# Two layers of attention and mixture of experts on one Trainium2 core: the second attention's output projected inside its own loop

## What is computed

```python
h = _layernorm(x) * (1 + ca) + sa
x = x + ga * _L1_attn_ref(h, w_qkvw, w_out)     # second layer's attention
h = _layernorm(x) * (1 + cb) + sb
x = x + gb * _L1_ffn_ref(h, Wr, br, W1, W2)     # one of 8 experts for each row

def _L1_attn_ref(x, w_qkvw, w_out):
    qkvw = x @ w_qkvw
    ...
    attn = jax.nn.softmax(q @ k.swapaxes(-2, -1) * scale, axis=-1)
    o = (attn @ v).swapaxes(1, 2).reshape(B, S, dim)
    return o * w.reshape(B, S, dim) @ w_out
```

## Time and profile before

| | |
|---|---|
| median of 3 executions | 2002.04 us (2001.77 to 2004.55) |
| the profiled execution | 2007.54 us, of which the span from first to last instruction is 2005.8 us |
| first attention and set-up | to 431 us |
| rows of the first layer, routing | 431 to 509 us |
| experts of the first layer | 509 to 1112 us |
| merge | to 1205 us |
| loop of the second attention | 1205 to 1588 us |
| tail and rows of the second layer | 1588 to 1691 us |
| routing, experts, end | 1691 to 2006 us |

### The profile page before, as it was taken

How to read it: one execution, slowest core, us unless ns; L and a number is a source line. 1 busy time by engine, 2 the same in 40 slices (tenths; PEclk the granted TensorE clock), 3 DMA queues, 4 the chain that set the end, 5 groups by cost and what they waited for, 6 DMA issues and landing times.

```text
span 2005.8 us, 32138 instructions
## 1 busy us (share of the span) xinstructions
PE 1682.2 (84%) x11048; PEld 1009.5 (50%) x11048; DVE 1160.1 (58%) x1885; ACT 861.2 (43%) x1909; POOL 1073.5 (54%) x901
## 2 busy tenths in 40 slices
PE   5699999976899999999999368777776476899992
PEld 3355555544466666666666233232231154677771
DVE  6798898876223223233233687999999687222214
ACT  3444444334344444444444374444342265444443
POOL 3377777623233323333332688999999764233322
PEclk8699999975899999999999678988888686899995
DMA  5013332018222223222241410000000275111115
GB/s 211 1 42 106 105 105 96 32 38 299 90 90 88 80 93 95 93 93 83 85 134 60 158 42 1 11 11 11 11 11 11 75 253 199 38 43 42 41 41 173
DMA packets 109286, 164.96 MB, mean 82 GB/s; under 512 B 27456, under 2 KB 74064, under 8 KB 109008
## 3 DMA queue, kind: packets, MB, share of 16 engines
q1 hardware_dynamic: 98960, 135.10, 19.7%
q0 software_dynamic: 10176, 27.80, 5.1%
HBM read 101.52 MB, written 61.34 MB: 81 GB/s over the span
## 4 chain that ended last, share of the span: by engine, by line
PE 62%; DVE 13%; POOL 12%; issue 5%; DMA 4%; ACT 3%; SPq 0%; POOLq 0%; DVEq 0%; ACTq 0%
PE ps L560 55%; POOL BIG L1832 11%; DVE BIG L1019 6%; PE ps L820 5%; ACT BIG L1511 2%; PE ps L792 1%; DVE bnst L1028 1%; DMA BIG<-OW 1%; DMA BIG<-YT 1%; DVE X L1019 1%; DMA HB<-BIG 1%; POOL X L1832 1%; DVE BIG L1433 1%; PE ps L675 1%; POOL BIG L1944 1%
## 5 line engine op out<-in xcount | busy, mean ns | idle before, releaser
L560 PE MATMUL ps<-BIG 128*128 (+8 forms) x8100 | 1326.3, 341 | 170.1 <-DVE BIG L1433 65.4
L560 PEld LDWEIGHTS ps<-BIG 128*128 128x128 f16 (+2 forms) x8100 | 744.0, 105 | 686.3 <-DVE BIG L1433 138.6
L1832 POOL TENSOR_TENSOR BIG<-BIG 128x256 f16<-128x256 f32 (+4 forms) x553 | 779.3, 1444 | 259.9 <-ACT BIG L1511 246.2
L1019 DVE TENSOR_TENSOR BIG<-ps,BIG 128x512 f32<-128x512 f32 (+3 forms) x725 | 477.2, 712 | 287.3 <-ACT BIG L1511 224.9
L1511 ACT ACTIVATE BIG<-ps 128x512 f16<-128x512 f16 (+5 forms) x1008 | 395.2, 445 | 535.4 <-PE ps L560 261.7
L1918 POOL DMA_INDIRECT YT<-BIG x106 | 105.1, 992 | 548.2 <-ACT BIG L1511 548.2
L1019 DVE TENSOR_TENSOR BIG<-BIG,ps 128x512 f32<-128x512 f32 (+1 forms) x204 | 120.9, 597 | 417.7 <-PE ps L560 401.8
L1511 ACT ACTIVATE BIG<-BIG 128x256 f16<-128x256 f32 (+2 forms) x354 | 208.8, 606 | 139.3 <-DVE BIG L1019 99.0
L1659 ACT ACTIVATE BIG<-ps 128x512 f32<-128x512 f32 x212 | 126.9, 599 | 137.5 <-PE ps L560 136.9
L1455 DVE TENSOR_REDUCE BIG<-BIG 128x160 f32<-128x2560 f32 x64 | 185.0, 2891 | 0.0
L1913 POOL DMA_INDIRECT BIG<-HB,BIG x106 | 103.1, 973 | 70.5 <-DVE BIG L1019 43.8
(11 more groups left out here) (118 smaller groups left out, 795.1 us busy)
## 6 DMA issues: line engine op xcount, KB each, us to landing
WD<-BIG SPq DMA_DIRECT2D x112, 256.0 KB, 2.3
BIG<-in_v SPq DMA_DIRECT2D x32, 512.0 KB, 5.0
BIG<-WD SPq DMA_DIRECT2D x32, 512.0 KB, 4.8
BIG<-in_w SPq DMA_DIRECT2D x24, 512.0 KB, 3.7
BIG<-WD SPq DMA_DIRECT2D x32, 384.0 KB, 7.3
BIG<-YT SPq DMA_DIRECT2D x24, 512.0 KB, 4.8
HB<-BIG SPq DMA_DIRECT2D x64, 128.0 KB, 3.3
X<-in_x SPq DMA_DIRECT2D x4, 1024.0 KB, 12.1
```

Source lines behind the costliest of these rows:

```text
L560: return e.matmul(o, lhsT, rhs, start=start, stop=stop, skip_group_check=True)
L1019: return e.tensor_tensor(o, a, b, op)
L1832: return e.tensor_tensor(o, a, b, op)
```

## The change

Of the 32 output tiles, 24 (six chunks of four) move from the tail into the loop, numbered n in the order in which chunks finish; the other 8 stay behind the loop in ticks 0 to 6 and 12 to 18 of `pre_tick(1, t)`. A tile takes other instructions now: PE turns it in float32 (`out_turn`), ACT takes the high half, PE subtracts it in PSUM (`out_less`), ACT takes the low half, PE projects it (`out_project`: six products with `w_out` already multiplied by the batch's gate, and one float32 product of `ident` with X that adds the old rows), and ACT copies the sum to X. POOL has no part in it, and DVE only measures it. The gated weights are made during the first layer's experts, eight halves-pairs of 512 columns; for this PE makes the gates in the first layer's `pre_tick` (`gate_pair`), and `convert_at` gives each step from 50 to 66 a conversion. In the loop, all four transposes of a chunk now stand in pass 5, and the 16 heads are spread over seven passes. The expert weights are loaded in pieces: 4 and 5 inside the loop, 6 at its end, 17 among the rows. The second layer's rows are taken in the chunks' order (`row_tile`).

```diff
         def convert_at(j):
-            if j < 56:
+            if j < 50:
                 return j // 2 if j % 2 == 0 else None
-            return j - 28 if j - 28 < N_CV[1] else None
+            return j - 25
...
-            return {8 * c - 10 + n: k for n, k in enumerate((3, 3, 3, 3, 2, 2))}
+            return {8 * c - 10 + n: k for n, k in enumerate((3, 3, 2, 2, 2, 2, 2))}
...
-            return {4: (0, 1), 5: (2, 3)}.get(q % 8, ()) if q < 56 else ()
+            return range(4) if q % 8 == 5 and q < 56 else ()
...
+        O_TURN, O_LESS, O_OUT, O_MEASURE = range(4)
+
+        def out_at(q, stage):
+            d = q - stage - 13
+            return [d // 2] if d >= 0 and d % 2 == 0 and d // 2 < N_IN else []
+
+        def late_at(t, stage):
+            return [n for n in range(N_IN, NT) if (n - N_IN if n < 28 else n - 28 + 12) + stage == t]
...
+            def gate_pair(p):
+                pe.wait_ge(s["modg"], 12)
+                if p == 3:
+                    pe.wait_ge(s["gb"], 1)
+                for b in (2 * p, 2 * p + 1):
+                    m = gate(1, 0, ps[1 + p % 3][:, 256 * (b % 2):], b)
+                m.then_inc(s["gb_ps"], 1)
...
             for t in range(NT + 6):
                 pre_tick(0, t)
+                if t in GATE_TICKS:
+                    gate_pair(GATE_TICKS.index(t))
...
+            def out_turn(n):
...
+                for kk in range(2):
+                    m = mm(out_banks(n)[0][:, 128 * kk:128 * kk + 128], OI[k][:, 128 * kk:128 * kk + 128], ident[:, :], kk == 0, False)
+            def out_less(n):
+                pe.wait_ge(s["o_hi"], n + 1)
+                mm(out_banks(n)[0], neg16[:, :], OIT[out_slot(n)[1]][:, 0].rearrange(FLAT), False, True).then_inc(s["o_ng"], 1)
+            def out_project(n):
...
+                for kk in range(2):
+                    for p, (a, b) in enumerate(HALVES):
+                        mm(o, ot[:, a, kk, :], w[:, b, kk, :], kk == 0 and p == 0, False)
+                mm(o, ident[:, :], X[:, out_tile(n), :], False, True).then_inc(s["pd_ps"], 1)
...
             for q in range(NQ):
                 less_max(q + 1)
+                for n in out_at(q, O_OUT):
+                    out_project(n)
                 for c, h in heads_at[q]:
                     project(c, h)
                 turn_qk(q // 8 + 1, turns_next(q))
+                for n in out_at(q, O_LESS):
+                    out_less(n)
                 scores(q + 2)
+                for n in out_at(q, O_TURN):
+                    out_turn(n)
...
                 values(q, 1)
                 sums(q - 1)
+                for n in out_at(q, O_MEASURE):
+                    out_measure(n)
...
+                    if l == 0 and (convert_at(j) or 0) >= C_OUT:
+                        out_weights_by_gate(convert_at(j))
```

More of the change, by code:

```diff
@@ L528, in sync @@
+            out_weights_in(7)
+            sp.wait_ge(s["s_ps"], NQ)
+            sp.wait_ge(s["pm"], pm_p[NQ - 1])
+            for i in (12, 13, 14, 15, 19, 20):
+                weights_in(1, i)
             heads_out(7)
-            sp.wait_ge(s["fin"], 16)
+            for n in range(3):
+                rows_out(1, n)
+            for n in range(28, 32):
+                out_in(n)
             sp.wait_ge(s["vr"], NQ)
             sp.wait_ge(s["mx_ps"], NQ)
-            router_in(1)
-            for t in range(6):
-                out_in(6 + t)
-                weights_in(1, t)
@@ L536, in sync @@
-            for t in range(NT + 6):
-                if 12 + t < NT:
-                    out_in(12 + t)
-                for k, i in steps(NT, 7, t):
-                    if k == 2:
-                        rows_out(1, i)
-            weights_in(1, 31)
+            sp.wait_ge(s["pd_ps"], N_IN)
+            sp.wait_ge(s["fin"], 16)
+            late = [6, 7, 8, 9, 10, 11, 18, 21, 22, 23, 24, 25, 26, 27, 28, 30, 31]
+            for n in range(3, NT):
+                rows_out(1, n)
+                if n % 2:
+                    weights_in(1, late.pop(0))
@@ L543, in sync @@
+            for i in late:
+                weights_in(1, i)
             for g in range(3):
@@ L996, in tensor @@
+            pe.wait_ge(s["e_sb"], NQ)
             pe.wait_ge(s["vr"], NQ)
-            pe.wait_ge(s["fin"], 16)
+            pe.wait_ge(s["qk"], 384)
+            pe.wait_ge(s["qt"], 32)
+            pe.wait_ge(s["wx"], N_IN)
             scale_rows(1, 0)
-            for t in range(6, 12):
-                tail_tick(t)
             for t in range(NT + 6):
-                if 12 + t < NT + 7:
-                    tail_tick(12 + t)
+                for n in late_at(t, O_OUT):
+                    out_project(n)
+                for n in late_at(t, O_LESS):
+                    out_less(n)
+                for n in late_at(t, O_TURN):
+                    out_turn(n)
@@ L1780, in scalar @@
                 powers(q + 1)
+                for n in out_at(q, O_OUT):
+                    out_x(n)
+                for n in out_at(q - 1, O_TURN):
+                    out_hi(n)
                 for c, h in heads_at[q]:
@@ L2022, in gpsimd @@
             finish(7, "weigh")
-            def tail_tick(t):
-                for st, i in steps(NT, 8, t):
-                    if st == 6 and i % 2 == 0:
-                        pool.wait_ge(s["wy"], i + 1)
-                        tt(X[:, i, :], X[:, i, :], YG1[i % 2], ALU.add).then_inc(s["wx"], 1)
-                    if st == 2:
-                        pool.wait_ge(s["o_hi"], i + 1)
-                        tt(OIP[i % 2][:, 1, :], OI[i % 4], OIP[i % 2][:, 0, :], ALU.subtract).then_inc(s["o_lo"], 1)
-            for t in range(12):
-                tail_tick(t)
-            pool.wait_ge(s["fin"], 16)
             for t in range(NT + 6):
-                if 12 + t < NT + 7:
-                    tail_tick(12 + t)
                 pre_tick(1, t)
```

311 lines of the change are left out of this document (176 added, 135 removed).

## The result

| | before | changed |
|---|---|---|
| median of 7 executions | 2002.04 us (1997.18 to 2005.63) | 2011.37 us (2007.98 to 2012.85) |
| the profiled execution, its span | 2007.54, 2005.8 us | 2012.52, 2010.4 us |
| first layer's rows, first to last | 37.0 us | 43.2 us |
| loop, first to last `top` | 369.6 us | 414.1 us |
| last reciprocal of the loop to routing | 103.4 us | 57.4 us |

The changed kernel is slower: the ratio of times is 1.0043, with a 95% interval of 1.0027 to 1.0059. The medians differ by 9.3 us, the two profiled executions by 5.0.

A forecast was written before the change was run, and what follows sets the result against it. POOL was taken to bound the loop, 96.92 us busy of 100, with the bound moving to PE and DVE. Tail -34.6, loop +34.8, first layer's rows +7 and experts' end +1.3 gave +8.5: median 2010.5 us, range 1978 to 2030.

The forecast's parts named there:

- first layer's rows (gates): First layer's rows: four gate pairs on PE, which has little room there, cost 7 us, between 3 and 8.3.
- The loop's five chunks (passes 13 to 52): Second attention's loop, where tiles and heads stand together: 53.7 us a chunk, 6.35 more, 31.8 us in all.
- four in pass 5 are 4.58: Loop, PE's chain in pass 5: transposes take 2.29 us per two, so all four take 4.58 of the pass's 8.6.
- Pass 3: Loop: 5.5 us at full clock; PE's 2.0 us waits in passes 2 and 4 counted once at half price, 1.1.
- POOL's 46 us a chunk hide the longer pass 5: Loop before tiles and heads stand together: POOL's work covers the longer pass 5, so no loss is counted there.
- The last eleven passes: End of the loop, with one set of transposes and no heads: a loss of 3 us.
- The tail: Last reciprocal of the loop to routing: 68.8 us instead of 103.4, a gain of 34.6, between 25.6 and 45.6.
- PE has no room beside them: Tail, ticks with the eight late tiles: PE cannot hide their 14 or 28 us, so 20 us is added.
- POOL stays the bound: Loop: POOL's lead absorbs the long pass 5, loop costs 6, sum -20, 1982 us; chance 0.2.
- The clock stays up: Loop and tail: more PE work keeps the clock at 1.00, sum -19.5, 1982.5 us; chance 0.18.
- The clock falls in most odd passes: Loop costs 51, tail gains 25.6, sum +34, 2036 us, or 2027 with a middling tail; chance 0.17.
- The tiles don't leave the tail: Loop: a load from OW comes late and PE waits there; time between the cases; chance 0.05.

The follow-up runs named there:

- experiment 3: Changed kernel with the four gate pairs in ticks 31 to 34 of the first layer's rows instead of 6, 12, 18 and 24: 2009.7 us, 1.0029.
- experiment 2: Kernel before with only the heads over seven passes and all four transposes in pass 5, no output tiles in the loop: 2018.34 us, 1.0093.
- experiment 5: Changed kernel with all 32 pieces of expert weights loaded among the second layer's rows, none in the loop: 2012.57 us, 1.0061.
- experiment 4: Changed kernel with ten unused PE products behind `scores` in each even pass from 14 to 60: 1997.14 us, 0.9977.
- experiment 7: Changed kernel with transposes split over passes 4 and 5, and unused PE products (22 in pass 0, ten in other even passes from 14 to 60): 1968.65 us, 0.9835.
- experiment 10: Kernel before with unused PE products behind `scores`, 22 in pass 0 and ten in other even passes from 14 to 60: 2005.45 us, 1.0015.
- experiment 1: Changed kernel with the heads again over six passes and the transposes two in pass 4, two in pass 5: 1986.85 us, 0.9918.

## Why the prediction was right, and where its terms were not

The forecast was +8.5 us with 2010.5 for the median; 2011.37 came. Its mechanism holds: a large gain in the tail, about as large a loss in the loop, and the gates tip the sum. Two terms were mis-sized by 10 and 11 us, and they cancel. That the forecast came within 1 us of the median is therefore luck; what it had right is the direction and the places of gain and loss.

| term | forecast | measured |
|---|---|---|
| first layer's rows (gates) | +7 | +6.2 in the rows, 5.6 at the experts' first transpose |
| end of the first layer's experts | +1.3 | +0.2 (with the gates +5.8 at the first `top`) |
| loop | +34.8 | +44.5 |
| last `top` to last reciprocal's end | not counted | +0.4 |
| tail | -34.6 | -46.0 |
| sum | +8.5 | +4.7 in the profiled pair, +9.3 in the medians |

**The loop's five chunks (passes 13 to 52), 31.8 forecast, 35.0 measured.** The method, each pass as the longer of two chains, gave every pass but three within 0.2 us. *Pass 5*, forecast 8.6, took 10.4: the step "four in pass 5 are 4.58" failed. The second pair follows the first through the same banks and waits 0.51 us for ACT, then takes 2.86 where the first takes 2.3 to 2.5; four are 5.82. The `scores` behind them ran at a low clock, 0.6 more. In experiment 3 one pass 5 ran at a clock of 1.00 from end to end: the four took 5.53 and the pass 9.5, so 0.95 of the 1.8 missing is the transposes themselves. Experiment 2 shows the same rows without tiles. *Pass 1*, forecast 7.7, took 7.0: the clock was low only for its first 3 to 4 us. *Pass 3*, put at a half chance of 2.2, lost its clock in four of five chunks here: 7.0, where 5.3 is what it takes with the clock up. In experiment 3, with the same loop, it never lost it and pass 5 did. By what these passes take with the clock up (5.3, 5.3 and 9.5) the clock cost 1.7, 1.7 and 0.9 us a chunk, 4.3 where 3.3 were forecast; in which passes it would fall no row had shown.

**Passes 5 to 12, forecast free, cost 1.5.** "POOL's 46 us a chunk hide the longer pass 5" failed: the chunk went from 47.57 to 49.04 us, and experiment 2 has the reason. A pass of 10 us leaves POOL waiting for the copies of those very transposes, so its lead does not help.

**The last eleven passes, forecast +3, cost 7.7 up to the last `top`.** The one long pass in them alone is 5.2 longer (1566.75 to 1577.05, 10.30 instead of 5.10); I had taken it at the price of the change in pace.

**The tail, forecast -34.6.** Three sizes were off. The start of the rows took 0.66 us, not 2.5: the square root's table load was not in the way. From the last row to the routing it was 7.7, not 9.3. The tiles cost 12.0, not 20. The step "PE has no room beside them" was too strict: where the clock was at 1.00, PE's four transposes of a row took 0.39 us instead of 0.59, which leaves some room. Experiment 5 adds that the 12.0 hold only with 15 pieces of weights loaded early; with all of them in the rows the tail takes 67.7 us. The result, -46.0, lies at the forecast's lower end, 45.6. That end is also what the Trainium skill's rule on PE-mode transposes ("TensorE: Matmul & The Clock Gate", Part 4) gave. The trace agrees in part: 0.75 in the window with tiles' plain products, 0.50 once only rows are left. But the tail's mean clock fell, from 0.76 before the change to 0.71 after it (each from the last reciprocal's end to the routing), so the clock was not what brought the gain. It was not tried to have tiles turned in transpose mode.

**The rivals.** *POOL stays the bound*: refuted, by its 8 us of wait, and by experiment 2 even where it had been the bound. *The clock stays up*: not so in the changed kernel (0.90 in the loop, as before), yet experiments 4, 7 and 10 show that the rival named the right resource: kept up, the clock is worth 14 us here, 17 to 18 with the split, and nothing before the change. *The clock falls in most odd passes*: it fell in pass 1, in pass 3 and at the end of pass 5, so more often than the forecast had it; the loop's 44.5 lies between the forecast's 34.8 and this rival's 51. *The tiles don't leave the tail*: 24 did, and nothing in the trace waits for a load from OW in the loop. Weights and DMAs as a bound of the rows, which the forecast excluded, are excluded by experiment 5 for the 17 pieces that stand there; all 32 would cost 10 us more.

What stays open: the 4.6 us between the difference of medians and that of the profiled pair, why the second pair of transposes takes 0.3 to 0.5 us more than the first, and what decides in which passes of a chunk the clock falls.

## What to carry to other kernels

When work moves into a loop, add each pass as the longer of the chains between two starts of the pacing instruction, and ask of every moved piece whether it stands inside the chain or in the gap behind it: a piece in the chain is paid even if every engine has room. A placing that was harmless beside one bound (all transposes in one pass) is the first thing to undo when the bound moves. And an engine that becomes the bound pays for its own idle times through its clock, so an idle time that cost nothing before is worth filling after.

## What the runs showed of the hardware

- Products that nobody reads made the kernel faster: 14 us in experiment 4, 17 to 18 in experiment 7 against experiment 1. In the kernel before, the products of experiment 7 gave nothing (3 to 4 us slower, experiment 10).
- Moving 24 measurements of 0.53 us each out of the loop into a stretch where nothing hides them made the kernel 7 to 9 us faster. PE's idle time in passes 2 and 4 fell from 2.05 to 1.51 us, and the loop's clock was higher (0.93 against 0.88 to 0.91 from 1300 to 1400 us).
- The same loop, with the same idle times, lost PE's clock at different places in different traces: mostly in passes 1 and 3 in the changed kernel's, in passes 1 and 5 in experiment 3's. The loop took 411 to 414 us either way.
- 16 products of 32x512 take 2.3 to 2.5 us as the first group and 2.8 to 2.9 right behind another such group, in the kernel before and in the changed one.
- SP's loads of 512 KB and stores of 128 KB together ran at 331 GB/s for 62 us; the 264 GB/s of the earlier trace rows, which the forecast used as the DMAs' rate, was no limit.
